# Handing the end of two token blocks to GpSimd in the tail of an adaLN attention and mixture-of-experts block

## The reference, cut to what matters

```python
h = layernorm(x) * (1 + ca) + sa
x = x + ga * attention(h)                # causal, one head, width 256
h = layernorm(x) * (1 + cb) + sb
# mixture: 16 experts, 4 chosen for each token, and one shared expert
moe_out = sum over the 4 chosen e of  cw[e] * (silu(h @ we1[e]) * (h @ we3[e])) @ we2[e]
shared  = (silu(h @ ws1) * (h @ ws3)) @ ws2
x = x + gb * (shared / 5 + moe_out * 4 / 5)
```

## Time and profile before

| what | value |
|---|---|
| median of 3 runs | 388.69 us |
| the runs | 388.35 to 391.52 us |
| span of the profiled execution | 345.7 us |
| median less span | 43.0 us |
| TensorE busy in the span | 96% |
| mean granted TensorE clock | 0.997 |

### The profile page before, as it was taken

How to read it: one execution, slowest core, us unless ns; L and a number is a source line. 1 busy time by engine, 2 the same in 40 slices (tenths; PEclk the granted TensorE clock), 3 DMA queues, 4 the chain that set the end, 5 groups by cost and what they waited for, 6 DMA issues and landing times.

```text
span 345.7 us, 7924 instructions
## 1 busy us (share of the span) xinstructions
PE 331.0 (96%) x2370; PEld 308.4 (89%) x2370; DVE 255.7 (74%) x793; ACT 196.9 (57%) x439; POOL 202.3 (59%) x278
## 2 busy tenths in 40 slices
PE   7999999999889999999999988999999999999995
PEld 6698999999889999988878877999999999998884
DVE  2989998789978887466898756666666665666986
ACT  2567877675766855665443315666666666665110
POOL 1678855331788777457777400666666666667700
PEclk9999999999999999999999999999999999999998
DMA  6415920000112259872322155787776664989734
GB/s 208 158 50 200 286 64 18 17 15 19 68 70 85 88 183 333 275 228 109 119 104 99 73 159 153 228 233 228 226 228 197 193 209 153 331 337 341 291 119 163
DMA packets 43353, 57.56 MB, mean 167 GB/s; under 512 B 6224, under 2 KB 35664, under 8 KB 43312
## 3 DMA queue, kind: packets, MB, share of 16 engines
q1 hardware_dynamic: 35360, 35.42, 34.0%
q0 software_dynamic: 6864, 19.80, 14.8%
q10 hardware_dynamic: 1088, 1.84, 1.5%
HBM read 32.64 MB, written 24.40 MB: 165 GB/s over the span
## 4 chain that ended last, share of the span: by engine, by line
PE 80%; DVE 10%; issue 5%; POOL 1%; DMA 1%; ACT 1%; DVEq 0%; POOLq 0%; ACTq 0%
PE ps L1700 18%; PE ps L1701 18%; PE ps L1702 18%; PE ps L1863 7%; PE ps L2061 5%; PE ps L2087 3%; PE ps L1874 2%; PE ps L1707 2%; PE ps L1897 2%; DMA cols<-in_L_c_dram 1%; PE ps L1800 1%; DVE bn L1118 1%; DVE gated L1368 1%; PE ps L1941 1%; PE ps L1785 1%
## 5 line engine op out<-in xcount | busy, mean ns | idle before, releaser
L729 POOL DMA_INDIRECT y_rows<-y_sb,aside x79 | 77.8, 985 | 54.3 <-ACT y_sb L1000 41.2
L694 POOL DMA_INDIRECT xg_rows<-hrow,slot_u x64 | 67.0, 1047 | 20.8 <-issue 17.8
L1700 PE MATMUL ps<-rpool 128*128 128x256 f32 (+3 forms) x228 | 68.7, 302 | 2.9 <-DVE rpool L1143 2.1
L1702 PE MATMUL ps<-rpool 128*128 128x256 f32 (+3 forms) x228 | 65.7, 288 | 0.0
L1701 PE MATMUL ps<-rpool 128*128 128x256 f32 (+3 forms) x228 | 65.7, 288 | 0.0
L1700 PEld LDWEIGHTS ps<-rpool 128*128 128x128 f32 x228 | 43.4, 190 | 4.9 <-DVE rpool L1143 3.1
L1700 PE MATMUL ps<-w_hi_routed,xT_hi 128*128 x158 | 45.1, 286 | 1.8 <-DVE xT_lo L1636 1.8
L1702 PE MATMUL ps<-w_hi_routed,xT_lo 128*128 x158 | 44.7, 283 | 0.0
L1701 PE MATMUL ps<-w_lo_routed,xT_hi 128*128 x158 | 44.6, 283 | 0.0
L1701 PEld LDWEIGHTS ps<-rpool 128*128 128x128 f32 x228 | 43.5, 191 | 0.5
L1702 PEld LDWEIGHTS ps<-rpool 128*128 128x128 f32 x228 | 43.4, 190 | 0.6
(11 more groups left out here) (224 smaller groups left out, 899.7 us busy)
## 6 DMA issues: line engine op xcount, KB each, us to landing
xs<-xg_rows SPq DMA_DIRECT2D x68, 144.0 KB, 2.4
y_in<-y_rows SPq DMA_DIRECT2D x16, 512.0 KB, 5.6
xg_rows<-empty SPq DMA_DIRECT2D x4, 576.0 KB, 3.4
x_in<-in_L_attn_x_dram SPq DMA_DIRECT2D x16, 128.0 KB, 2.2
w_raw_routed<-in_L_ffn_we_dram SPq DMA_DIRECT2D x8, 256.0 KB, 4.0
out_dram<-x SPq DMA_DIRECT2D x16, 128.0 KB, 1.8
xs_own<-xg_rows SPq DMA_DIRECT2D x11, 144.0 KB
wmod_sb<-in_L_wmod_dram ACTq DMA_DIRECT2D x3, 512.0 KB, 6.2
```

The source lines that it names most:

```text
L694: nc.gpsimd.indirect_dma_start(out=xg, out_offset=bass.IndirectOffsetOnAxis(ap=slot_u[:, t, k:k + 1].bitcast(U32), axis=0), in_=hrow[:, t, ...
L729: nc.gpsimd.indirect_dma_start(out=yb, out_offset=bass.IndirectOffsetOnAxis(ap=dest[:, 2 * n + i:2 * n + i + 1].bitcast(U32), axis=0), in_ ...
L1700: nc.tensor.matmul(dst, w[0], x_[0], start=first, stop=False)
L1702: return nc.tensor.matmul(dst, w[1], x_[0], start=False, stop=last)
```

## The change

It deals the sums of the tail out anew:

- **GpSimd**, behind its last send, adds place 3 of block 0, scales block 0 and finishes it, and then finishes block 1: four instructions of 128 x 1024.
- **VectorE** loses these four and gets two: it now adds places 1 and 2 of block 3 to place 0, which makes one sum of three places. `SUMS` lists the order of its ten adds, so that others can wait for the one they need.
- **TensorE** makes two place sums for block 3, of the summed place 0 and of place 3, both behind `gate_up(15)`; before it made four.
- **SyncE** stores block 0, then block 2, then block 1, then the first three tiles of block 3. **ScalarE**'s queue stores the last tile.

```diff
@@ -104,6 +104,9 @@
 
 
 TAIL = 3
+
+
+SUMS = ((0, 1), (1, 1), (0, 2), (1, 2), (2, 1), (NB - 1, 1), (NB - 1, 2), (2, 2), (1, 3), (2, 3))
 
 
 def slot_of(t):
@@ -458,7 +461,11 @@
             "xT", "xhi", "xlo", "gate_up", "silu", "g", "gT", "ghi", "glo", "down", "y"))
         s_yin = [[sem(f"y_in{k}_{b}") for b in range(NB)] for k in (1, 2, 3)]
         s_mark_const, s_marks = sem("mark_const"), sem("marks")
-        s_sum, s_scaled, s_done = sem("sums"), sem("rows_scaled"), sem("tiles_done")
+        s_sum, s_scaled, s_done, s_ended = sem("sums"), sem("rows_scaled"), sem("tiles_done"), sem("ended_by_pool")
+
+        def summed_by(b, k):
+
+            return SUMS.index((b, k)) + 1
 
         x_t = x.rearrange("b (i p) d -> b i p d", p=P)
         out_t = out.rearrange("b (i p) d -> (b i) p d", p=P)
@@ -593,13 +600,13 @@
                     first = (1 + k) * T + b * TB
                     sp.dma_start(whole(b)[k], yb[first:first + TB, :].rearrange("(p t) d -> p t d", t=BT)
                                  ).then_inc(s_yin[max(k, 1) - 1][b], 16)
-            for b in range(NB - 1):
-                sp.wait_ge(s_done, b + 1)
+            for b, ended, count in ((0, s_ended, 3), (2, s_done, 1), (1, s_ended, 4)):
+                sp.wait_ge(ended, count)
                 for t in range(b * BT, (b + 1) * BT):
                     sp.dma_start(out_t[t], x1[:, t, :]).then_inc(s_out, 16)
             for i in range(2):
-                sp.wait_ge(s_done, NB + i)
-                for t in range((2 * NB - 2 + i) * BT // 2, (2 * NB - 1 + i) * BT // 2):
+                sp.wait_ge(s_done, 2 + i)
+                for t in range((2 * NB - 2 + i) * BT // 2, (2 * NB - 1 + i) * BT // 2 - i):
                     sp.dma_start(out_t[t], x1[:, t, :]).then_inc(s_out, 16)
             for r in range(RING):
                 sp.wait_ge(s_back[r], 16 * loads_of(NPAIR - RING + r))
@@ -729,6 +736,24 @@
                     nc.gpsimd.indirect_dma_start(
                         out=yb, out_offset=bass.IndirectOffsetOnAxis(ap=dest[:, 2 * n + i:2 * n + i + 1].bitcast(U32), axis=0),
                         in_=y_sb[:, r, i, :], in_offset=None).then_inc(s_back[r], 16)
+
+            def tokens(b):
+                return x1[:, b * BT:(b + 1) * BT, :]
+
+            first = whole(0)
+            pool.wait_ge(s_sum, summed_by(0, 2))
+            pool.wait_ge(s_yin[2][0], 16)
+            nc.gpsimd.tensor_tensor(first[0], first[0], first[3], ALU.add).then_inc(s_ended, 1)
+            pool.wait_ge(s_gb, 1)
+            pool.wait_ge(s_ended, 1)
+            nc.gpsimd.tensor_tensor(first[0], first[0], gate_b[:, 0:1, :].broadcast_to((P, BT, D)), ALU.mult
+                                    ).then_inc(s_ended, 1)
+            pool.wait_ge(s_shared, 1)
+            pool.wait_ge(s_ended, 2)
+            nc.gpsimd.tensor_tensor(tokens(0), tokens(0), first[0], ALU.add).then_inc(s_ended, 1)
+            pool.wait_ge(s_shared, 2)
+            pool.wait_ge(s_scaled, 1)
+            nc.gpsimd.tensor_tensor(tokens(1), tokens(1), whole(1)[0], ALU.add).then_inc(s_ended, 1)
 
 
         @block.scalar
@@ -1016,6 +1041,8 @@
 
             for n in range(UNITS_FIRST + 1, UNITS_SH):
                 silu_step(n)
+            act.wait_ge(s_done, 3)
+            act.dma_start(out_t[TILES - 1], x1[:, TILES - 1, :]).then_inc(s_out, 16)
 
 
         @block.vector
@@ -1405,7 +1432,7 @@
 
                 mine = x1[:, b * BT:(b + 1) * BT, :]
                 dve.wait_ge(s_shared, b + 1)
-                dve.wait_ge(s_scaled, b + 1)
+                dve.wait_ge(s_scaled, b)
                 nc.vector.tensor_tensor(mine, mine, whole(b)[0], ALU.add).then_inc(s_done, 1)
 
             def last_shared(i):
@@ -1671,20 +1698,18 @@
                     g_rows_lo(n - 1)
             add_place(0, 1)
             add_place(1, 1)
-            add_place(2, 1)
             add_place(0, 2)
             g_step(UNITS_FIRST + 1)
             add_place(1, 2)
+            add_place(2, 1)
+            add_place(NB - 1, 1)
+            g_step(UNITS_FIRST + 2)
+            add_place(NB - 1, 2)
             add_place(2, 2)
-            add_place(0, 3)
-            scale(0)
-            finish(0)
             add_place(1, 3)
-            g_step(UNITS_FIRST + 2)
+            g_step(UNITS_FIRST + 3)
             scale(1)
-            finish(1)
             add_place(2, 3)
-            g_step(UNITS_FIRST + 3)
             scale(2)
             finish(2)
             last_shared(0)
@@ -1861,18 +1886,20 @@
                     tok = slice(j * P, (j + 1) * P)
 
                     last = nc.tensor.matmul(to, unit(n)[1][:, tok], w_raw_s[:, e, W2:WX],
-                                            start=(e == 0 and b < NB - 1 and j % 2 == 0), stop=(e == SH - 1),
+                                            start=(e == 0 and j % 2 == 0), stop=(e == SH - 1),
                                             skip_group_check=True)
                 if BT - 1 in tiles or n == UNITS_SH - 1:
                     last.then_inc(s_y, 1)
 
-            def place_sum(k, first):
-
-
-                pe.wait_ge(s_yin[max(k, 1) - 1][NB - 1], 32 if k < 2 else 16)
+            def place_sum(k):
+
+                if k == 0:
+                    pe.wait_ge(s_sum, summed_by(NB - 1, 2))
+                else:
+                    pe.wait_ge(s_yin[k - 1][NB - 1], 16)
                 for j in range(BT):
                     nc.tensor.matmul(ps[:, 4 + j // 2, j % 2 * D:(j % 2 + 1) * D], ident[:],
-                                     y_in[k][:, (NB - 1) * BT + j, :], start=(first and j % 2 == 0), stop=False,
+                                     y_in[k][:, (NB - 1) * BT + j, :], start=False, stop=False,
                                      skip_group_check=True)
 
             for s in range(FIRST, LAST + 1):
@@ -2125,14 +2152,12 @@
 
             gate_up(UNITS_FIRST + 1)
             pe.wait_ge(s_ry, NPAIR)
-            place_sum(0, True)
-            place_sum(1, False)
-            place_sum(2, False)
             down(UNITS_FIRST)
             gate_up(UNITS_FIRST + 2)
             down(UNITS_FIRST + 1)
             gate_up(UNITS_FIRST + 3)
-            place_sum(3, False)
+            place_sum(0)
+            place_sum(3)
             for half in (range(0, BT // 2), range(BT // 2, BT)):
                 down(UNITS_FIRST + 2, half)
                 down(UNITS_FIRST + 3, half)
```

## The result

| what | before | after |
|---|---|---|
| median of 6 runs | 388.59 us | 396.87 us |
| the runs | 387.94 to 392.55 us | 393.60 to 399.05 us |
| ratio, 95% interval | | 1.0186 (1.0152 to 1.0221) |
| span of the profiled execution | 345.7 us | 391.9 us |
| time of that execution | not given | 393.6 us |

The change costs 7.2 us (5.9 to 8.6: the ratio and the ends of its interval, times 388.59; the two medians alone lie 8.3 apart); 395.1, or +6.4, was forecast. The profile of one experiment, e6, fell in a slow run, so that only durations of its instructions are read, not its span.

A forecast was written before the change was run, and what follows sets the result against it. The prediction took TensorE to bound the tail, with VectorE 1.4 us behind. A finish of block 2 later by 4.97 us plus 1.42 for stores made +6.4, so 388.69 became 395.1 us, range 392.0 to 398.0.

The forecast's parts named there:

- exclusion by whole instructions: Tail: two-input VectorE instructions and GpSimd's take turns on SBUF, each for a whole instruction; 395.1 us, chance 0.56.
- exclusion in pieces: Rival: in the tail the engines exclude each other in pieces of some 256 columns; +5.7, 394.4 us, chance 0.12.
- Up to 327.3 us nothing waits: Start of the tail: VectorE and TensorE run without new waits until GpSimd starts its add at 327.30.
- GpSimd's instruction at 2.34 us: Tail: cost of one 128 x 1024 GpSimd instruction, extended linearly from 256 columns; bounds 1.22 and 2.94 us.
- what would show it: Signs in the tail's profile: four or five VectorE instructions at 3.0 to 3.5 us, GpSimd's at 2.3 or some 3.2.
- ... there is a gap into which a waiting GpSimd steps: Tail: nearly every VectorE instruction waits on a semaphore for its predecessor, which lets a waiting GpSimd in.
- The finish of block 2, +4.97: Tail: VectorE's finish of block 2 ends at 345.02 in place of 340.05, 4.97 us later.
- Eleven stores for eight, +1.42: SyncE's queue behind the finish of block 2: three more stores at 0.473 us each, 1.42 us.
- The sum, +6.4: Whole kernel: 4.97 us for the finish of block 2 plus 1.42 us for stores, 6.4 us slower.
- The same 43.0 around it: Outside the profiled span: the 43.0 us between span and time stay unchanged, so 352.1 us of span gives 395.1.
- side by side: Rival: at this size the two engines don't exclude each other in the tail; 387.4 us, chance 0.14.
- the dear GpSimd: Rival: a GpSimd instruction in the tail costs its upper bound of 2.94 us; +8.8, 397.5 us, chance 0.08.

The follow-up runs named there:

- e6: Against e1: only the finish of block 1 moved to GpSimd, with the stores in after's order; 1.0092 of before.
- e2: Against after: GpSimd's four instructions cut to one column each, leaving out nearly all their sums, with waits and stores kept; 0.9954 of before.
- e3: Against after: GpSimd's four instructions replaced by iota fills that write the same places and read nothing, sums left out; 0.9973 of before.
- e5: Against after: each of GpSimd's four instructions cut in four of 256 columns, with the same sums; 1.0148 of before.
- e7: The after kernel run again without an edit, in another group than the first after; 1.0157 of before.
- e8: Against after: GpSimd's four instructions replaced by multiplications by one with a single input, sums left out; 1.0023 of before.
- e0: The before kernel run and profiled again without an edit; 1.0014 of before.
- e4: Against after: block 1's four stores moved from SyncE's queue to ScalarE's, ahead of its last tile; 1.0113 of before.
- e1: Against after: GpSimd's four instructions given back to VectorE, blocks stored in the order 0, 1, 2; 1.0079 of before.

## Why the prediction was right

It named exclusion by whole instructions as the cause, and after, e2, e3, e5 and e6 show it for instructions of two inputs. The time alone wouldn't: exclusion in pieces was put at +5.7, only 0.7 us from the forecast. Step by step, its walk against the rows of after (less 39.29):

| step of the prediction | predicted | measured |
|---|---|---|
| GpSimd starts | 327.30 | 327.91 |
| (3,2) ends | 330.76 | 331.41 |
| (2,2) ends | 334.12 | 334.71 |
| (1,3) ends | 337.48 | 337.98 |
| TensorE stands for `g_step` 15 | 2.7 us | 2.59 us |
| TensorE ends | 340.7 | 341.49 |
| GpSimd's finish of block 1 ends | 342.60 | 343.05 |
| finish of block 2 ends | 345.02 | 345.47 |
| last `last_rows` ends | 347.76 | 348.11 |
| span ends | 352.1 | 352.6 |

- **Up to 327.3 us nothing waits**: the one step with an error of its own. VectorE's `g_step` 13 and 14 came at 322.79 and 327.25, as worked out, but the last send began at 326.92 where it had been at 326.20, so GpSimd was ready 0.6 us later. Its effect stayed small, since it only shifts the turns, as the prediction said of this case; in e7 it shifted them onto other adds. The cover of 0.3 us ahead of `place_sum(0)` was gone with it, and became a wait of 0.42.
- **GpSimd's instruction at 2.34 us**: 2.40 alone, and 2.2 to 2.3 of its own where it waited first. The linear step from 256 columns and one held, and four times the 256 columns (4 x 0.733 = 2.93; the prediction has 2.94) didn't. Its lower bound was mis-summed too: four turns at 1.22 in place of 2.34 take 4.5 us from the +6.4, which leaves +1.9 and not +2.4.
- **In turns, with whole instructions**: a pair of one VectorE and one GpSimd instruction takes 374.00 - 370.70 = 3.30 us; 2.34 + 1.22 - 0.2 = 3.36 was used. Four VectorE instructions were recorded at 3.56, 3.20, 3.18 and 3.25 and three of GpSimd's at 3.16, 3.14 and 3.19, as "what would show it" had it. The Trainium skill ("SBUF — State Buffer", "SBUF: two separate sides") says that of a VectorE instruction with two SBUF inputs and a GpSimd one that reads SBUF, whichever starts first gets the pair of ports for the whole instruction; the section that the prediction names has the two-input case, but says "for the whole instruction" of another mode. For GpSimd's form with two inputs, the rows above now agree at this size. For its form with one input they don't: in e8 VectorE was held for 0.76 of 2.63 us, and the measurement decides.
- **"... there is a gap into which a waiting GpSimd steps"**: the gap isn't needed. In e7 GpSimd got in twice between VectorE instructions of which the second didn't wait for the first.
- **The finish of block 2, +4.97**: measured +5.42 for after against the first profile of before, +5.02 for e7 against e0.
- **Eleven stores for eight, +1.42**: B rose by 1.49 and 1.46, and e4 took 1.7 away.
- **The sum, +6.4**: the tails give 34.1 - 27.2 = +6.9 and 34.8 - 28.3 = +6.5 (paired the other way, 5.8 and 7.6), the times +7.2 (5.9 to 8.6) and, in e7, +6.3 (4.9 to 7.6, from 1.57% of 398.8).
- **"The same 43.0 around it"** was wrong as a reading: some 41 of the 43.0 us lay in the middle of the span, in which the timed runs were slower than the profiled one. It did no harm, since the premise was used on both sides and the change touches the tail alone. A change in the routed loop could not have been costed in that way.

Of the rivals, side by side is refuted by after's own rows; exclusion in pieces came only where the instructions were cut (e5, which measured 1.0148; the 394.4 of the prediction would be 1.0147), and the dear GpSimd is refuted by its 2.40.

**Where the loss comes from.** With the data taken from GpSimd the rest of the change gains 1.3 to 2.4 us in the tail (e2 against before and e0). GpSimd's work on whole blocks adds 8.1 to A (27.0 against e2's 18.9) and thus to the whole. With all the work done every variant measured slower than before (e1, e4, e5, e6), e1 the least, by 0.79%: VectorE and TensorE end within 1.4 us of each other there, so work moved off one is at once behind the other, and the third engine didn't take VectorE's sums without stopping it. e2's time would be a gain only if the work that it leaves out cost nothing.

## What to carry to other kernels

Before handing VectorE's elementwise work to an idle GpSimd, look in the trace for meetings of the two. If VectorE's instructions with two SBUF inputs are longer there, each two-input instruction handed over that meets one saves VectorE 1.22 us and costs it nearly GpSimd's whole duration (here 2.0 us). What didn't hold VectorE up in these runs was a GpSimd instruction beside one of VectorE's with an input in PSUM, and a GpSimd instruction that only wrote; one that read a single array held it for 0.76 us. Cutting GpSimd's instructions small frees VectorE, but then GpSimd itself waits and ends late (e5). And compare profiles by the stretch that the change touches, with before profiled twice: spans of the same kernel were 42 us apart here.

## What the runs showed of the hardware

- A fill of 128 x 1024 float32 by GpSimd (`iota`) took 1.00 us and didn't hold VectorE at all (e3).
- A GpSimd instruction of 128 x 1024 with two inputs lengthened a VectorE instruction with two SBUF inputs by 2.0 to 2.3 us (after).
- One with one input kept VectorE out for 0.76 us, a fixed stretch in four meetings, and worked on for 1.9 us beside it (e8).
- A one-column instruction of GpSimd took 0.19 us, and 0.99 and 1.04 where it met a VectorE add (e2).
- The wait is inside the record: a "busy" engine may be one that stands for the other. GpSimd's 11.9 us of records in the tail of after (2.40 + 3.16 + 3.14 + 3.19) hold some 9 us of work.
- A stretch of the routed experts ran at 171 matmul records in 20 us in one execution of before, at 138 in another and at 128 in one of after. What sets this pace is open.
